# Inverse standard deviations of three layer normalisations: GpSimd's addition and power in place of ScalarE's square root and VectorE's inversion

## What is computed

```python
def _layernorm(x, axis=-1, eps=1e-05):
    m = jnp.mean(x, axis=axis, keepdims=True)
    v = jnp.var(x, axis=axis, keepdims=True)
    return (x - m) / jnp.sqrt(v + eps)
...
x = _layernorm(x + self_attention(x))          # 16 heads of 8, 1024 rows of 128
x = _layernorm(x + cross_attention(x, ctx))    # 6404 keys, masked
x = _layernorm(x + experts(x))                 # one of 8 experts for each row
```

## Time and profile before

| | |
|---|---|
| executions timed | 505.09, 508.35, 509.07 us |
| median | 508.35 us |
| profiled execution, span from first to last instruction | 505.4 us |
| TensorE busy | 482.0 us, 95% |
| VectorE busy | 419.7 us, 83% |
| ScalarE busy | 368.0 us, 73% |
| GpSimd busy | 209.5 us, 41% |

### The profile page before, as it was taken

How to read it: one execution, slowest core, us unless ns; L and a number is a source line. 1 busy time by engine, 2 the same in 40 slices (tenths; PEclk the granted TensorE clock), 3 DMA queues, 4 the chain that set the end, 5 groups by cost and what they waited for, 6 DMA issues and landing times.

```text
span 505.4 us, 13819 instructions
## 1 busy us (share of the span) xinstructions
PE 482.0 (95%) x4122; PEld 197.3 (39%) x4122; DVE 419.7 (83%) x612; ACT 368.0 (73%) x718; POOL 209.5 (41%) x316
## 2 busy tenths in 40 slices
PE   7999999999999999987999999999999999999983
PEld 2433333333333344632344444444444444433641
DVE  5999999999999926668699989999899899831766
ACT  6358888888888875441678877877878887787263
POOL 4825755885469900132233323333233332320045
PEclk9899999999999999999799999999999999999997
DMA  4859864875453014524133110111111111010101
GB/s 116 350 147 305 280 219 166 298 259 194 167 173 137 12 54 123 161 62 121 42 71 81 41 40 26 40 37 30 38 32 40 40 40 40 27 40 22 43 1 45
DMA packets 21772, 52.58 MB, mean 104 GB/s; under 512 B 5021, under 2 KB 13375, under 8 KB 19649
## 3 DMA queue, kind: packets, MB, share of 16 engines
q1 hardware_dynamic: 18461, 22.46, 16.8%
q0 software_dynamic: 2304, 28.84, 15.4%
q10 hardware_dynamic: 932, 0.37, 0.3%
HBM read 42.10 MB, written 8.94 MB: 101 GB/s over the span
## 4 chain that ended last, share of the span: by engine, by line
PE 81%; DVE 9%; ACT 5%; issue 3%; DMA 1%; SPq 0%; DVEq 0%; POOL 0%; ACTq 0%; POOLq 0%
PE O L1321 32%; PE ST L1555 15%; PE RT L1527 10%; PE ST L1352 10%; PE RT L1338 5%; DVE mxs L786 3%; ACT prob L1102 2%; PE O L1292 1%; DVE mxc L937 1%; PE RT L1231 1%; ACT Vx L1180 1%; PE O L1317 1%; PE RT L1464 1%; ACT prob L1141 1%; PE RT L1679 1%
## 5 line engine op out<-in xcount | busy, mean ns | idle before, releaser
L937 DVE TENSOR_REDUCE mxc<-RT 128x1024 f32 (+1 forms) x192 | 196.1, 1045 | 23.4 <-PE RT L1527 18.9
L1141 ACT ACTIVATE prob<-ST 128x512 f32<-128x512 f32 x320 | 172.4, 596 | 38.7 <-PE ST L1555 36.8
L1102 ACT ACTIVATE prob<-ST 128x512 f32<-128x512 f32 x256 | 138.6, 597 | 24.7 <-PE ST L1352 14.1
L786 DVE TENSOR_REDUCE mxs<-RT 128x2 f32<-128x1024 f32 x128 | 152.7, 1224 | 2.8 <-PE RT L1338 0.6
L1527 PE MATMUL RT<-Kr,Qs 64*128 64x128 f32 (+1 forms) x512 | 121.8, 375 | 2.7 <-DVEq L924 1.2
L1555 PE MATMUL ST<-Qs,Kc 64*128 64x512 f32 x320 | 122.3, 458 | 2.0 <-DMA Qs<-qd_x 1.4
L1321 PE MATMUL O<-prob,vst 128*9 128x256 f32 x1280 | 100.3, 385 | 1.7 <-ACT prob L1141 1.3
L1338 PE MATMUL RT<-Kself,Qs 64*128 64x512 f32 x256 | 89.6, 454 | 1.8 <-DVE Kself L753 0.9
L1352 PE MATMUL ST<-Qs,Kself 64*128 64x512 f32 x256 | 91.2, 450 | 0.0
L1321 PE MATMUL O<-prob,Vs 128*9 128x256 f32 x1024 | 79.3, 381 | 1.5 <-ACT prob L1102 0.7
L1555 PEld LDWEIGHTS ST<-Qs,Kc 64*128 64x128 f32 x320 | 54.5, 187 | 61.2 <-issue 31.6
(11 more groups left out here) (232 smaller groups left out, 355.4 us busy)
## 6 DMA issues: line engine op xcount, KB each, us to landing
big<-in_mask POOLq DMA_DIRECT2D x16, 1760.0 KB, 7.3
big<-kd SPq DMA_DIRECT2D x66, 80.0 KB
od_s<-osb SPq DMA_DIRECT2D x14, 128.0 KB, 1.9
od_x<-osb SPq DMA_DIRECT2D x14, 128.0 KB, 1.8
Qs<-qd_s SPq DMA_DIRECT2D x12, 128.0 KB, 6.3
Qs<-qd_x SPq DMA_DIRECT2D x12, 128.0 KB, 3.8
qd_s<-Vx SPq DMA_DIRECT2D x2, 512.0 KB, 4.8
qd_x<-big SPq DMA_DIRECT2D x2, 512.0 KB, 4.5
```

Of the source, the lines that this page charges most:

```text
L786: v.tensor_reduce(mxs[:, h % 2, c2, :].rearrange("p (f t) -> p f t", f=2)[:, :, q], RT[r % 2][:, :].rearrange("p (f k) -> p f k", f=2), AX ...
L937: v.tensor_reduce(o, src, AX.X, ALU.max).then_inc(S("x_row_free"), 1)
L1102: nc.scalar.activation(prob[:, c % SLOTS, k * HALF:(k + 1) * HALF], ST[(2 * c + k) % 3][:, :], ACT.Exp) \
L1141: nc.scalar.activation(prob[:, b, (k % 2) * HALF:(k % 2 + 1) * HALF], ST[BANK[k]][:, :], ACT.Exp) \
```

## The change

The square root on ScalarE, its table loads and VectorE's inversion go away. GpSimd gets two instructions for each half, on 128 x 4 values: variance plus eps (a TENSOR_SCALAR), and that to the power of minus one half (a TENSOR_TENSOR with a tile that holds -0.5). Both add to the semaphore `*_std`, and the power waits for the addition.

```diff
+        half = sb("half", [P, 4])
-            g_.memset(eps[:, :], EPS).then_inc(S("cst"), 1)
+            g_.memset(half[:, :], -0.5).then_inc(S("cst"), 1)
...
+            def inverse_std(a, h):
+                w = slice(4 * h, 4 * h + 4)
+                pool.wait_ge(S(a + "_var"), 4 * h + 4)
+                g_.tensor_scalar(rstd[:, w], mv[:, w, 1], EPS, None, ALU.add).then_inc(S(a + "_std"), 1)
+                pool.wait_ge(S(a + "_std"), 2 * h + 1)
+                g_.tensor_tensor(rstd[:, w], rstd[:, w], half[:, :], ALU.pow).then_inc(S(a + "_std"), 1)
+
+            for h in range(2):
+                inverse_std("s", h)
             pool.wait_ge(S("vx_ones"), 1)
...
+            for h in range(2):
+                inverse_std("x", h)
             step = 5
...
                 if h:
+                    inverse_std("f", 0)
                     step = four_experts(4, 6)
                     step = four_experts(6, 7)
                     step = four_experts(7, 8)
...
                     g_.tensor_tensor(be_rows[h], be_rows[h], e_sum[:, 4:8, :], ALU.add).then_inc(S("bias_in"), 1)
+                    inverse_std("f", 1)
...
             def normalised(a, h, o, name):
                 w = half_of(h)[0]
-                dve.wait_ge(S(a + "_std"), h + 1)
-                ch(v.reciprocal(rstd[:, w], rstd[:, w]))
+                dve.wait_ge(S(a + "_std"), 2 * h + 2)
...
-            def std(a, h):
-                act.wait_ge(S(a + "_var"), 4 * h + 4)
-                act.wait_ge(S("cst"), 8)
-                w = slice(4 * h, 4 * h + 4)
-                nc.scalar.activation(rstd[:, w], mv[:, w, 1], ACT.Sqrt, bias=eps[:, 0:1]).then_inc(S(a + "_std"), 1)
...
-            act.preload_act_table(ACT.Sqrt)
-            for h in range(2):
-                std("s", h)
-            act.preload_act_table(ACT.Exp)
             turned_x("s")
...
-            act.preload_act_table(ACT.Sqrt)
-            std("x", 0)
             turned_half(0)
-            std("x", 1)
-            act.preload_act_table(ACT.Exp)
             router_exp(0)
...
-            act.preload_act_table(ACT.Sqrt)
             expert_biases(0)
...
             expert_parts(3, 0)
-            std("f", 0)
             expert_parts(3, 1)
             biases_out(1)
-            std("f", 1)
```

More of the change, by code:

```diff
@@ L108, in decoder_layer @@
         rowk = sb("rowk", [P, 12])
-        eps = sb("eps", [P, 1])
+        half = sb("half", [P, 4])
         Qs = sb("Qs", [P, HEADS, HALF], F32R)
```

## The result

| | before | after |
|---|---|---|
| executions timed | 22 | 22 |
| median | 506.4 us | 508.39 us |
| lowest to highest | 504.31 to 509.07 us | 506.71 to 511.89 us |
| ratio to before (95% interval) | | 1.0041 (1.0024 to 1.0059) |
| profiled execution, span | 505.4 us | 505.7 us |

The change makes the kernel slower by 0.41%, that is 2.1 us (1.2 to 3.0). That is within 1%, where the forecast had put it, but three times the forecast shift of 0.67 us. That the predicted 509.0 us lies near the 508.39 us is luck, of two things that cancel: more executions of the kernel before brought its median down from 508.35 to 506.4 us, and the change cost more than forecast.

What follows compares the result with a forecast made beforehand. TensorE's attention products bound most of the kernel; the change acts on three short normalisation passages. Terms -0.39 + 0.11 + 0.60 + 0.35 = +0.67 us, added to the median 508.35, gave 509.0 us, range 504.8 to 516.5.

Steps and rivals of the forecast that it cites:

- The place of the loss: Three normalisation passages on the chain, with hand-overs among VectorE, ScalarE and GpSimd; shifts -0.39, +0.11, +0.60 and +0.35 us.
- The formula for each passage: Variance to normalisation takes 0.43 us plus the power's time; today 0.58 us at the last normalisation's second half.
- p = 0.5: GpSimd's power over four columns: estimated at 0.5 us, from a 0.20 us row for 128 x 8 values.
- p = 0.2: Low end for the power's time, from the cheapest two-input GpSimd instruction of about this size; sum -0.23 us.
- The hand-overs and the addition: From variance to normalisation through GpSimd, without the power: 0.05 + 0.19 + 0.09 + 0.10 = 0.43 us.
- The whole 1.28 us is lost in GpSimd's queue: Last normalisation, first half: GpSimd's tree waits behind addition and power, so the removed load gains nothing; +0.60 us.
- VectorE itself is early: Last normalisation, first half: it starts at about 494.55 instead of 495.48, and the rest of VectorE's work follows.
- The table load at 1.28 us: One load on the chain, between tile 3's last weighted part and the router weights' copy: priced at 1.28 us, no drain.
- x1 covered: Second half of cross-attention's normalisation: some 0.3 us later, hidden by 0.78 us of cover ahead of TensorE.
- No stretching of s0's normalisation beside the power: First normalisation, first half: the power beside it adds nothing; by the shared-interface rule up to 0.42 us per normalisation.
- The slow power: Rival: GpSimd's power takes several us; +5.1 us at 1.5 us, about +39 at 7.13; chance 0.25.
- the gain come through: Rival: the table load's saving reaches the end because GpSimd's tree isn't late; up to -1.5 us, 506.9; chance 0.05.

Runs made afterwards that it cites:

- the tree first: The changed kernel with GpSimd's tree for tiles 4 and 5 ahead of the addition and power of the last normalisation's first half: 508.32 us, ratio 1.0044.
- two powers: The changed kernel with a second power of the same shape ahead of the first in each pair, into an unread tile: 517.25 us, ratio 1.0222.
- the idle time filled: The kernel with two powers, with 23 in place of 14 idle TensorE products ahead of cross-attention's first transposes: 516.67 us, ratio 1.0202.

## Why the prediction was right, and where it was off

- *The place of the loss*: right. The formula for each passage holds. With 1.04 for p its terms are +0.14, +0.65, +1.14 and +0.89, sum +2.8. The profile has +0.15, +0.74, +0.95 and +0.88, and the timed ratio 2.1 (1.2 to 3.0). At f0 it is 0.19 less because the load was worth 1.47 us and not 1.28.
- *p = 0.5, "two and a half times that row"*: the term that was mis-sized. It is 1.04 us, five times the row. All of the difference between 0.67 and 2.8 is this one number, multiplied by the four places at which it lies open. The multiplication in its place brought the passages to -0.36, where the prediction had -0.23 for p = 0.2.
- *The hand-overs and the addition, 0.43 us in all*: right. At f1 from the variances' end to the normalisation it is 1.47 us, 0.43 + 1.04.
- *"The whole 1.28 us is lost in GpSimd's queue"*: lost it is, but not in the queue alone. GpSimd's idle 1.34 us ahead of the pair (1.30 forecast) and the wait for L683 are as forecast, and with the load moved in the kernel before 1.42 us came through. But the step "VectorE itself is early", with the rest of its work following, failed: f0's normalisation started 0.57 us earlier and not 0.93, took 1.04 us longer beside the tree, and the addition behind it came 0.47 us later. The prediction weighed such a stretching at "s" and not here. With the tree first, 0.39 us of loss stayed.
- *The table load at 1.28 us*: a little low. With no load between them ScalarE's copy starts 0.13 us before the last part ends (485.47 against 485.60); with the load it started 1.32 us behind it (488.49 against 487.17). The load also breaks that overlap. The Trainium skill (ScalarE: Activation LUTs, What ACT_TABLE_LOAD costs) has 2.66 us for a switch, drain included. The 1.47 us up to L681, and the 1.42 us with the load moved, stand against it: no drain of 1.38 us is seen here.
- *x1 covered*: right for one power (11.65 against 11.64 us), not for two.
- *No stretching of s0's normalisation beside the power*: right. Its four take 1.08 us beside L637 and L639, 1.11 before. The Trainium skill (GPSIMD Engine Reference, Key points) has GpSimd and VectorE share their SBUF interfaces. The stretching at f0, beside the tree, agrees with that; beside a power over four columns none shows.
- *The slow power* (over 1.5 us) did not come about, nor did the gain come through. The argument against the slow power, that 32 values a partition cost no more than 0.2 us in any simple row, isn't read from GpSimd: rows over 128 x 32 that take 0.19 us are VectorE's, and GpSimd's nearest are copies over 128 x 27, 0.21 us (L572).

## What to carry to other kernels

Before an operation moves to another engine, count how often it will lie open on the chain, since its price is multiplied by that; an engine for which the trace shows no such function needs that one price measured before anything else. A table load needn't go away: here, in a place where its engine waited 1.24 us anyway, it cost next to nothing, and moving it took one line. What is put at the head of a queue holds up all that is ready behind it, and what is held up then starts beside other work and can slow it: here a saving ahead of the queue was lost to both.

## What the runs showed of the hardware that I had not expected

- GpSimd's power on fp32 takes about 385 ns + 158 ns for each column of 128 values: 0.54, 0.70, 1.04, 1.63 and 2.89 us for 1, 2, 4, 8 and 16 columns.
- VectorE's normalisation of f0, four instructions of 0.34 us alone, took 2.26 us beside GpSimd's tree before and 3.30 after, where both start together (3.28 with the multiplication, 2.49 with the tree first); single ones reached 1283 ns.
- TensorE's granted clock fell to 1.2 GHz behind idle times of 1.92, 1.44 and 0.82 us in some profiled executions, and stayed at 2.4 GHz behind equal ones of 1.44 and 0.83 us in others. Where it fell, products took 1.7 to 1.9 times as long (3.31 and 3.76 us in place of 1.96, 2.08 in place of 1.12), until it rose again some 3 to 7 us later. With two powers the time from the copy of x0 to ScalarE's first part was 8.03 us, and 6.12 with the idle time filled: a wait added ahead of TensorE cost more than its length.
